# A recurrence with input gate and candidate by one tanh, the state by a two-element scan, and a last tanh without pointer operands

## What is computed

```
i_t = sigmoid(xi_t + h @ V_i)
g_t = tanh(xg_t + h @ V_c)
o_t = sigmoid(xo_t + h @ V_o)
c_new = h * c + i_t * g_t
h_new = o_t * tanh(c_new)
```

## Time and profile before

| | us |
|---|---|
| median of 3 runs | 2955.86 |
| lowest, highest | 2954.85, 2957.86 |
| the profiled execution | 2956.47 |
| its span, first to last instruction | 2954.8 |
| mean granted TensorE clock | 0.569 of full |

### The profile page before, as it was taken

How to read it: one execution, slowest core, us unless ns; L and a number is a source line. 1 busy time by engine, 2 the same in 40 slices (tenths; PEclk the granted TensorE clock), 3 DMA queues, 4 the chain that set the end, 5 groups by cost and what they waited for, 6 DMA issues and landing times.

```text
span 2954.8 us, 67705 instructions
## 1 busy us (share of the span) xinstructions
PE 1386.3 (47%) x20258; PEld 998.8 (34%) x20258; DVE 1920.9 (65%) x15110; ACT 1449.6 (49%) x8446; POOL 169.7 (6%) x130
## 2 busy tenths in 40 slices
PE   4989867444444444444444444444444444444433
PEld 4434422333333333333333333333333333333322
DVE  6557788666666666666666666666666666666666
ACT  5431123455555555555555555555555555555554
POOL 0530066000000000000000000000000000000000
PEclk8999978555555555555555555555555555555555
DMA  6010000000000000000000000000000000000000
GB/s 251 1 36 1 0 0 6 2 2 2 2 1 2 1 2 2 2 2 2 2 2 2 2 2 2 2 2 2 1 2 2 2 2 2 2 2 2 2 2 16
DMA packets 12829, 26.80 MB, mean 9 GB/s; under 512 B 1971, under 2 KB 9654, under 8 KB 10422
## 3 DMA queue, kind: packets, MB, share of 16 engines
q1 hardware_dynamic: 10406, 22.02, 2.1%
q10 hardware_dynamic: 2064, 0.55, 0.1%
HBM read 21.52 MB, written 1.05 MB: 8 GB/s over the span
## 4 chain that ended last, share of the span: by engine, by line
ACT 43%; PE 30%; DVE 17%; issue 9%; DMA 1%; SPq 0%; POOL 0%; DVEq 0%; POOLq 0%; ACTq 0%
ACT work L667 25%; PE psum L500 15%; DVE work L990 12%; ACT work L658 12%; ACT psum L660 5%; PE psum L504 5%; PE psum L419 4%; PE psum L360 2%; PE psum L371 1%; DVE work L902 1%; DMA work<-in_adj_dram 1%; DVE FT L939 1%; PE psum L399 1%; PE psum L290 1%; DVE X L946 0%
## 5 line engine op out<-in xcount | busy, mean ns | idle before, releaser
L500 PE MATMUL psum<-work,MASK 128*128 128x1 f16 x12288 | 814.9, 169 | 1443.1 <-DVE work L990 1429.0
L500 PEld LDWEIGHTS psum<-work,MASK 128*128 128x128 f16 x12288 | 647.3, 108 | 1630.3 <-DVE work L990 1629.2
L658 ACT ACTIVATE work<-psum 128x1 f32<-128x1 f32 x2048 | 350.7, 171 | 1139.4 <-PE psum L504 1139.4
L667 ACT ACTIVATE work<-psum,work 128x2 f32<-128x2 f32 x2048 | 722.4, 353 | 2.8 <-issue 2.8
L504 PE MATMUL psum<-work,MASK 128*128 128x1 f16 x6144 | 710.7, 172 | 0.0
L987 DVE TENSOR_SCALAR work<-work 128x1 f32<-128x1 f32 x2048 | 315.5, 154 | 527.1 <-ACT work L662 527.1
L504 PEld LDWEIGHTS psum<-work,MASK 128*128 128x128 f16 x6144 | 543.2, 104 | 0.0
L990 DVE TENSOR_TENSOR_SCAN work<-work 128x3 f16<-128x3 f32 x2048 | 341.5, 167 | 279.2 <-ACT work L667 5.9
L1000 DVE SCALAR_TENSOR_TENSOR work<-psum,work 128x1 f32<-128x1 f32 x2048 | 433.4, 212 | 0.0
L1003 DVE TENSOR_TENSOR work<-work 128x1 f32<-128x1 f32 x2048 | 325.8, 159 | 70.5
L662 ACT ACTIVATE work<-psum 128x2 f32<-128x2 f32 x2048 | 354.8, 173 | 0.0
(11 more groups left out here) (142 smaller groups left out, 1061.4 us busy)
## 6 DMA issues: line engine op xcount, KB each, us to landing
work<-in_adj_dram SPq DMA_DIRECT2D x16, 1024.0 KB, 5.0
work<-in_L_ffn_Wd_dram SPq DMA_DIRECT2D x4, 512.0 KB, 6.2
out_dram<-work SPq DMA_DIRECT2D x4, 256.0 KB, 2.4
work<-in_L_ffn_bd_dram SPq DMA_DIRECT2D x1, 512.0 KB, 6.8
W<-in_L_ffn_W_dram ACTq DMA_DIRECT2D x1, 256.0 KB, 2.8
watt<-in_L_gnn_w_att_dram ACTq DMA_DIRECT2D x2, 64.0 KB, 6.9
work<-in_L_gnn_Wq_dram SPq DMA_DIRECT2D x1, 64.0 KB, 9.3
Wfc<-in_L_gnn_W_fc_dram ACTq DMA_DIRECT2D x1, 64.0 KB, 5.5
```

The source lines that it names most:

```text
L500: nc.tensor.matmul(into, Vparts[:, gate, part, :], h_steps[:, q, 2:3], start=False, stop=False, skip_group_check=True)
L658: nc.scalar.activation(sig_i[:, q], bank(NGATE * k)[:, col:col + 1], ACT.Sigmoid, scale=1.0 / SCALE_V).then_inc(i_ready, 1)
L667: nc.scalar.activation(Z[:, t % 2, 0:3:2], bank(6 + t % 2)[:, 0:1].to_broadcast([P, 2]), ACT.Tanh, bias=hc[:, q], scale=sig_i[:, q]).then_ ...
```

## The change

The sigmoid is replaced by sigmoid(s) = (1 + tanh(s/2)) / 2. V, U and the bias of the gates i and o are halved once ahead of the loop, so that all three gates are plain tanh of their sums. Then, with I = tanh(s_i/2) and G = g:

- ScalarE makes I and G in one instruction over two elements (L668 of the changed kernel), reading one column of two neighbouring PSUM banks into IG.
- VectorE makes twice the new state by a scan of two elements (L998): it begins at 1.0, and its first element is I * 1 + 1 = 1 + I; the second is (1 + I) * G + 2 h c. The addends are CADD, 1.0 and the product of h and the doubled state. The scan writes into PSUM, bank 6 or 7. No separate c is made any more, and L1014 is h times the doubled state.
- ScalarE makes tanh(0.5 * doubled state), with an immediate scale and no bias operand (L674).
- The output gate is a tanh into SBUF (L671); VectorE makes (1 + tanh)/2, written twice, and minus that (L1001, L1003).
- TensorE does the rounded parts of i and g first, then both remainders, then o.

The diff, without declarations:

```diff
                     pe.wait_ge(h_ready, t + 1)
-                    gate_sum(0, i_summed)
-                    gate_sum(1, g_summed)
-                    gate_sum(2, o_summed)
+                    rounded(0, 1)
+                    rounded(0, 0)
+                    rounded(1, 1)
+                    rounded(1, 0)
+                    pe.wait_ge(low_ready, t + 1)
+                    remainder(0)
+                    remainder(1).then_inc(ig_summed, 1)
+                    rounded(2, 1)
+                    rounded(2, 0)
+                    remainder(2).then_inc(o_summed, 1)
...
-                    act.wait_ge(i_summed, t + 1)
-                    nc.scalar.activation(sig_i[:, q], bank(NGATE * k)[:, col:col + 1], ACT.Sigmoid, scale=1.0 / SCALE_V).then_inc(i_ready, 1)
-                    act.wait_ge(g_summed, t + 1)
-                    nc.scalar.activation(bank(6 + t % 2)[:, 0:1], bank(NGATE * k + 1)[:, col:col + 1], ACT.Tanh, scale=1.0 / SCALE_V).then_inc(g_ready, 1)
+                    act.wait_ge(ig_summed, t + 1)
+                    nc.scalar.activation(IG[:, q, 0:2], psum[:, NGATE * k:NGATE * k + 2, col], ACT.Tanh,
+                                         scale=1.0 / SCALE_V).then_inc(ig_ready, 1)
                     act.wait_ge(o_summed, t + 1)
-                    nc.scalar.activation(Z[:, t % 2, 3:8:4], bank(NGATE * k + 2)[:, col:col + 1].to_broadcast([P, 2]),
-                                         ACT.Sigmoid, scale=1.0 / SCALE_V).then_inc(o_ready, 1)
-
-                    act.wait_ge(g_ready, t + 1)
-                    act.wait_ge(hc_ready, t + 1)
-                    nc.scalar.activation(Z[:, t % 2, 0:3:2], bank(6 + t % 2)[:, 0:1].to_broadcast([P, 2]), ACT.Tanh,
-                                         bias=hc[:, q], scale=sig_i[:, q]).then_inc(tanh_ready, 1)
+                    nc.scalar.activation(o_tanh[:, q:q + 1], bank(NGATE * k + 2)[:, col:col + 1], ACT.Tanh,
+                                         scale=1.0 / SCALE_V).then_inc(o_ready, 1)
+                    act.wait_ge(c_ready, t + 1)
+                    nc.scalar.activation(Z[:, q, 0:3:2], bank(6 + q)[:, 1:2].to_broadcast([P, 2]), ACT.Tanh,
+                                         scale=0.5).then_inc(tanh_ready, 1)
...
+            for w in (V, U, gate_bias):
+                chain.step(v.tensor_scalar(w[:, 0:NGATE:2, :], w[:, 0:NGATE:2, :], 0.5, None, ALU.mult))
...
-            v.memset(hc[:, 0:1], 0.0).then_inc(hc_ready, 1)
+            chain.step(v.memset(CADD[:, :, 0:1], 1.0))
+            v.memset(CADD[:, 0, 1:2], 0.0).then_inc(hc_ready, 1)
...
+                dve.wait_ge(ig_ready, t + 1)
+                dve.wait_ge(hc_ready, t + 1)
+                v.tensor_tensor_scan(bank(6 + q)[:, 0:2], IG[:, q, 0:2], CADD[:, q, 0:2], 1.0,
+                                     ALU.mult, ALU.add).then_inc(c_ready, 1)
                 dve.wait_ge(o_ready, t + 1)
-                v.tensor_scalar(z[:, 5:6], z[:, 3:4], -1.0, None, ALU.mult).then_inc(o_negated, 1)
+                v.tensor_scalar(z[:, 3:8:4], o_tanh[:, q:q + 1].to_broadcast([P, 2]), 0.5, 0.5,
+                                ALU.mult, ALU.add).then_inc(o_halved, 1)
+                v.tensor_scalar(z[:, 5:6], o_tanh[:, q:q + 1], -0.5, -0.5, ALU.mult, ALU.add).then_inc(o_halved, 1)
 
                 dve.wait_ge(tanh_ready, t + 1)
-                v.tensor_tensor_scan(h_steps[:, 1 - t % 2, 0:3], z[:, 2:5], rounding, 1.0,
+                dve.wait_ge(o_halved, 2 * t + 2)
+                v.tensor_tensor_scan(h_steps[:, r, 0:3], z[:, 2:5], rounding, 1.0,
                                      ALU.mult, ALU.add).then_inc(h_ready, 1)
-
-                dve.wait_ge(o_negated, t + 1)
...
                 v.tensor_tensor(h, z[:, 2:3], z[:, 3:4], ALU.mult).then_inc(state_ready, 1)
-
-                dve.wait_ge(hc_ready, t + 1)
-                v.scalar_tensor_tensor(c_[:, q], bank(6 + t % 2)[:, 0:1], sig_i[:, q], hc[:, q],
-                                       ALU.mult, ALU.add).then_inc(state_ready, 1)
-                dve.wait_ge(state_ready, 2 * t + 2)
-                v.tensor_tensor(hc[:, r], h, c_[:, q], ALU.mult).then_inc(hc_ready, 1)
+                dve.wait_ge(state_ready, t + 1)
+                v.tensor_tensor(CADD[:, r, 1:2], h, bank(6 + q)[:, 1:2], ALU.mult).then_inc(hc_ready, 1)
```

More of the change, by code:

```diff
@@ L146, in build_program @@
         SMALL = N
-        c_, hc, sig_i = (region(SMALL + 2 * k, 2) for k in range(3))
+        o_tanh = region(SMALL, 2)
+        IG = region(SMALL + 2, 4, "p (q s) -> p q s", q=2)
         h_low = region(SMALL + 6, 1).bitcast(FP16)
@@ L152, in build_program @@
         Z = region(SMALL + 24, 16, "p (q s) -> p q s", q=2)
+        CADD = region(SMALL + 40, 4, "p (q s) -> p q s", q=2)
         v_max = region(SMALL + 46, 1)
@@ L202, in build_program @@
         v_split, rec_start = sem("v_split"), sem("rec_start")
-        i_summed, g_summed, o_summed = sem("i_summed"), sem("g_summed"), sem("o_summed")
-        i_ready, g_ready, o_ready, tanh_ready = sem("i_ready"), sem("g_ready"), sem("o_ready"), sem("tanh_ready")
-        o_negated, h_ready, low_ready = sem("o_negated"), sem("h_ready"), sem("low_ready")
+        ig_summed, o_summed = sem("ig_summed"), sem("o_summed")
+        ig_ready, c_ready, o_ready, tanh_ready = sem("ig_ready"), sem("c_ready"), sem("o_ready"), sem("tanh_ready")
+        o_halved, h_ready, low_ready = sem("o_halved"), sem("h_ready"), sem("low_ready")
         state_ready, hc_ready = sem("state_ready"), sem("hc_ready")
@@ L495, in _, with into, rounded, remainder @@
                     k, col, q = t // HALF % 2, t % HALF, t % 2
[L497 to L505, removed]
-                    pe.wait_ge(h_ready, t + 1)
-                    gate_sum(0, i_summed)
-                    gate_sum(1, g_summed)
-                    gate_sum(2, o_summed)
+                    def into(gate):
+                        return bank(NGATE * k + gate)[:, col:col + 1]
+                    def rounded(gate, part):
+                        return nc.tensor.matmul(into(gate), Vparts[:, gate, part, :], h_steps[:, q, 2:3],
+                                                start=False, stop=False, skip_group_check=True)
+                    def remainder(gate):
+                        return nc.tensor.matmul(into(gate), Vlow[:, gate, :], h_low[:, q:q + 1],
+                                                start=False, stop=True, skip_group_check=True)
+                    pe.wait_ge(h_ready, t + 1)
+                    rounded(0, 1)
[8 more added lines that the diff above has]
+                    remainder(2).then_inc(o_summed, 1)
                     if t - col + HALF < N and col in (2, 4, 6):
@@ L514, in _ @@
                         gate_inputs(1 - k, col // 2 - 1, t - col + HALF)
-            pe.wait_ge(state_ready, 2 * N)
+            pe.wait_ge(state_ready, N)
             for c in range(NCH):
@@ L652, in _ @@
             root(NT)
-            nc.scalar.preload_act_table(ACT.Sigmoid)
+            nc.scalar.preload_act_table(ACT.Tanh)
             copy_ft(3, b0=6)
             for t in range(N):
-                    k, col, q = t // HALF % 2, t % HALF, slice(t % 2, t % 2 + 1)
-                    act.wait_ge(i_summed, t + 1)
-                    nc.scalar.activation(sig_i[:, q], bank(NGATE * k)[:, col:col + 1], ACT.Sigmoid, scale=1.0 / SCALE_V).then_inc(i_ready, 1)
-                    act.wait_ge(g_summed, t + 1)
-                    nc.scalar.activation(bank(6 + t % 2)[:, 0:1], bank(NGATE * k + 1)[:, col:col + 1], ACT.Tanh, scale=1.0 / SCALE_V).then_inc(g_ready, 1)
-                    act.wait_ge(o_summed, t + 1)
-                    nc.scalar.activation(Z[:, t % 2, 3:8:4], bank(NGATE * k + 2)[:, col:col + 1].to_broadcast([P, 2]),
-                                         ACT.Sigmoid, scale=1.0 / SCALE_V).then_inc(o_ready, 1)
-                    act.wait_ge(g_ready, t + 1)
-                    act.wait_ge(hc_ready, t + 1)
-                    nc.scalar.activation(Z[:, t % 2, 0:3:2], bank(6 + t % 2)[:, 0:1].to_broadcast([P, 2]), ACT.Tanh,
-                                         bias=hc[:, q], scale=sig_i[:, q]).then_inc(tanh_ready, 1)
+                    k, col, q = t // HALF % 2, t % HALF, t % 2
+                    act.wait_ge(ig_summed, t + 1)
+                    nc.scalar.activation(IG[:, q, 0:2], psum[:, NGATE * k:NGATE * k + 2, col], ACT.Tanh,
+                                         scale=1.0 / SCALE_V).then_inc(ig_ready, 1)
+                    act.wait_ge(o_summed, t + 1)
+                    nc.scalar.activation(o_tanh[:, q:q + 1], bank(NGATE * k + 2)[:, col:col + 1], ACT.Tanh,
[3 more added lines that the diff above has]
+                                         scale=0.5).then_inc(tanh_ready, 1)
         @block.vector
@@ L983, in _ @@
             for t in range(N):
-                z, q, r = Z[:, t % 2, :], slice(t % 2, t % 2 + 1), slice(1 - t % 2, 2 - t % 2)
+                z, q, r = Z[:, t % 2, :], t % 2, 1 - t % 2
                 h = HH[:, t:t + 1]
```

(10 more changed lines are left out.)

## The result

The changed kernel takes 3010.82 us (median of 4, 3009.72 to 3011.71) against 2956.86 for the kernel before: a ratio of 1.0183 (1.0165 to 1.02). It is slower by 54 us, 1.8%. Slower was forecast and the range held, but the forecast had 15 us. The profiled execution has a span of 3009.7 us, 54.9 more than before.

What follows compares the result with a forecast made beforehand. The recurrence's dependence cycle, 1181 ns a step, was taken to bound the kernel. Terms -25 + 17 + 161 + 34 - 180 = +7 ns, times 2048, plus 1.1 us once, gave +15.4 us: 2971 us, range 2942 to 3020.

Steps and rivals of the forecast that it cites:

- The cycle, and that no engine bounds: Recurrence loop: no engine is full; a dependence cycle through VectorE, TensorE and ScalarE sets 1181 ns a step.
- TensorE's order, -25: TensorE's sums: wait for the remainder moves from third to fifth matmul, so the sixth starts at 155 ns, not 180.
- The first tanh +17: First ScalarE instruction of the step: tanh over two elements takes 173 ns in place of 156.
- the last -180: Last tanh on ScalarE: without per-partition scale and bias it takes 173 ns in place of 353.
- Handovers of 34: From a result to the instruction waiting for it: 34 ns, VectorE to ScalarE included; one more on the cycle.
- S = 161: Duration of VectorE's new two-element scan into PSUM, between gates and last tanh: 161 ns, bounds 145 and 212.
- Once: Ahead of the loop: halving V, U and the bias adds 1.0 us, a memset 0.1, together +1.1 us.
- In both new places the second semaphore ... is the early one, so again nothing: Both VectorE scans waiting for two semaphores: the second is already there, so the extra wait costs the cycle nothing.
- The typical step, +7: Sum of all terms on one step of the loop's cycle: +7 ns.
- Rival C: A new wait on the cycle costs 17 to 40 ns a step: 3006 to 3053 us; chance 12%.
- Rival A: VectorE writes PSUM quickly, new scan 145 to 152 ns: faster, 2939 to 2953 us; chance 23%.
- B: VectorE writes PSUM slowly, new scan 212 ns: step grows by 58, 3076 us; chance 10%.

Runs made afterwards that it cites:

- old_order: Changed kernel with TensorE's order of before (remainder of i third, then the rounded parts of g): 3061.19 us, 1.0354 of the kernel before.
- scan_sbuf: Changed kernel with the doubled state written to SBUF in place of PSUM: 3055.45 us, 1.0339 of the kernel before.
- one_wait: Changed kernel with one semaphore wait in place of two at each VectorE scan, eight VectorE instructions a step: 2982.52 us, 1.0097 of the kernel before.
- waits_swapped: Changed kernel with the two waits at both scans named in the other order, late semaphore in the small instruction: 3295.94 us, 1.1153 of the kernel before.
- one_wait_ten: Changed kernel with one wait for each scan plus two one-element memsets, ten VectorE instructions a step again: 2981.95 us, 1.009 of the kernel before.
- before_one_wait: Kernel before with one semaphore at its last tanh, so ScalarE's small wait instruction goes: 2953.32 us, 0.9986 of the kernel before.

## Why the prediction was right or wrong

- **The cycle, and that no engine bounds: right.** Every experiment's time follows from its step on this cycle.
- **TensorE's order, -25: right.** 180 to 155 or 156 ns in the trace; old_order gives 27 back in the typical step, 25 in the mean.
- **The first tanh +17, the last -180: right.** 172 ns each, in place of 156 and 353: +16 and -181.
- **Handovers of 34: right to 2 ns.** Averaged over some 900 ordinary steps of the trace they are 32 (L668 to L998), 33 (L998 to L674, VectorE to ScalarE) and 32 (L674 to L1007).
- **S = 161: the first term that was mis-sized.** It is 170. For SBUF I had 164 and it is 163; the step that failed is "I stay near the reads ... and take a fifth of the 15". VectorE's write to PSUM costs 7 more instead of giving 3. Neither its reads nor ScalarE's writes told that. The error of 9 is those 3 and 7, less the 1 that the 164 was too high. These 9 ns on a step are 18 us. The Trainium skill (VectorE: DVE Perf Modes, The TRN2 errata) lists 62 cycles more for PSUM sources. The traces don't bear that out for small instructions: VectorE's product of h and the state takes 155 ns with the state in PSUM and 159 with it in SBUF (scan_sbuf).
- **"Once", +1.1: not seen.** The three halvings took 2.97 us in the trace, three times what I had. But VectorE waited 4.9 us for ScalarE ahead of the first step and still waits 4.7 us, so there is cover; it was in the trace and I didn't look for it. The first L990 started at 529.3 us and so does the first L1007. That they agree so well is in part luck: one_wait, with the same work ahead of the loop, starts its first one at 525.6 us, so one pair can't show 1 us.
- **"In both new places the second semaphore ... is the early one, so again nothing": wrong, and the larger part.** One half holds: the early semaphore is in the small instruction and it costs the typical step nothing (waits_swapped shows what the other order costs, 135 ns; the margin at L1007 was 2 to 3 ns all the same, not 50, because the 65 ns behind a small wait were missing in my working). What I missed is what that instruction does to an engine's stops every 128 instructions: 14.6 ns a step, 28 to 30 us. It was to be seen in the kernel before: L667 had 2.8 us of "issue", in 16 steps, and I passed over a number that small. On ScalarE it showed in one place of five; VectorE, twice on the cycle and held twice a step, shows it in five of five.
- **The typical step, +7, became +14:** nine more for S and two less in all the other terms, none of which is off by more than 3 ns.
- **Rival C** had the mechanism in half a sentence ("a wait for two semaphores delays the instruction behind it"), as a delay of every step; it had 12%. The measured 3010.8 lies in its stretch, 3006 to 3053. Rival A (a fast write to PSUM) is excluded by scan_sbuf, and B (S at 212) by the 170 in the profile. The measured time is outside the forecast's own 2963 to 2984; it is in the range only because that was stretched over C's lower half. That it came out slower is no luck: the typical step alone makes it so, by 29 us.

Together: the typical step grew by 14.2 ns (1193.3, the mean of one_wait, which has no long steps, less 1179.1, the mean of the kernel before without its 16), or 29.1 us. The long steps are 1207.9 - 1193.3 or 29.9 us, less the 3.8 us that the kernel before had already. That makes 55.2, and the spans differ by 54.9. Of the 40 us by which the forecast was off, 26 are the long steps and 15 the typical step.

What stays open is the stop itself. That it has to do with the fetch of the program is inferred, not shown; I did not change the size of what is fetched. The traces say this much. Of the two queues that the page calls "instruction", q14 moves packets of 8192 bytes, and two VectorE instructions fewer in each of 2048 steps (4096 in all) make 32 packets fewer (218 to 186), one for 128. In the changed kernel such a packet starts 0.63 to 0.96 us behind the start of each 128th VectorE instruction (all 151 between 560 and 2900 us); in one_wait it starts 1.3 to 1.6 us ahead of it (all 123). So the same boundary is met earlier, against the engine's own work, where there is no small wait, as the theory has it. But where the stop shows, the packet starts when the stop is over, so the stop isn't the time of that transfer.

That the small wait exposes the stop is shown on VectorE, by taking it away in the changed kernel and by adding one in the kernel before. For ScalarE it is not shown: the stops lie right behind L666, but the run that took L666 away also moved the 128th instruction to a place that never showed one.

## What to carry to other kernels

In a cycle of small instructions count, besides durations, the waits: here a second semaphore on an instruction was an instruction of its own, and on VectorE it cost time even where it was long satisfied. Where two producers can't overtake the step, let both count up one semaphore and wait for the sum; where two waits must stay, name the late one first. And compare the typical step with the mean before trusting either: here nearly half of the loss lay in one step of thirteen.

## What the runs showed that I had not expected

- The stop of an engine's instruction stream: 128 instructions apart, 417 ns from a small wait to the next VectorE instruction (67 in ordinary steps), and not to be seen in any of 2047 steps where neither engine has a small wait (one_wait, one_wait_ten, before_one_wait; on ScalarE before_one_wait tries one place alone).
- Behind a small wait the next VectorE instruction needs 64 to 65 ns, so a late semaphore there costs that much more than in the instruction itself.
- ScalarE reads two elements from SBUF 32 ns slower than from PSUM (204 against 172), VectorE writes PSUM 7 ns slower than SBUF (170 against 163).
